# One clear instead of two behind every second indirect transfer of GpSimd, in two expert layers

## What is computed

```python
h = patches(x)                                    # 4096 x 256
h = h + attention0(layernorm(h))
h = h + experts0(layernorm(h))                    # 7 routed experts, top 2, and a shared one
h = h + attention1(layernorm(h))
h = h + experts1(layernorm(h))                    # 16 experts in 4 groups, top 4
# experts: combine[t, e] is the weight of expert e for token t, zero but for the chosen ones
out = 0
for e in range(E):
    out = out + combine[:, e:e+1] * ((silu(x @ w_gate[e]) * (x @ w_up[e])) @ w_down[e])
```

## Time and profile before

| | |
|---|---|
| runs | 1649.97, 1649.74, 1642.79 us; median 1649.74 |
| profiled execution, its own time | 1643.09 us |
| span of its profile, first to last instruction | 1641.3 us |
| mean granted TensorE clock | 0.924 of full speed |
| PE busy | 1390.6 us, 85% of the span |
| DVE, ACT, POOL busy | 1049.6, 757.0 and 661.7 us |
| clears of layer 0 (L620) | 112, 14.4 us busy |
| clears of layer 1 (L1250) | 224, 26.4 us busy |
| indirect transfers of layer 1 (L1256, L1275) | 112 scatters and 112 gathers |

### The profile page before, as it was taken

The page is one execution under the profiler, slowest core; times in us unless marked ns, Lnnn a source line. Parts: engine busy times, 40 slices in busy tenths (PEclk is TensorE's granted clock), DMA queues, the critical chain, the costliest instruction groups (busy, mean ns, idle before and its releaser), DMA issues. The chain is left out here.

```text
span 1641.3 us, 37317 instructions
## 1 busy us (share of the span) xinstructions
PE 1390.6 (85%) x14157; PEld 1222.5 (74%) x14188; DVE 1049.6 (64%) x2196; ACT 757.0 (46%) x1288; POOL 661.7 (40%) x888
## 2 busy tenths in 40 slices
PE   6979999999999976688962788899767899889882
PEld 5867888888888866688862576667567889889882
DVE  4654575476476477765665468888758766466654
ACT  5324444444444433254541566677522365556520
POOL 4015312112111005466264354333365666663665
PEclk9989999999999997899995899999857999999997
DMA  7305655325325005247651010000082377877843
GB/s 278 116 27 169 224 168 190 105 87 190 111 91 172 2 5 215 78 148 238 207 174 37 14 33 8 1 2 2 2 307 71 113 254 236 259 232 232 240 126 90
DMA packets 142885, 215.59 MB, mean 131 GB/s; under 512 B 14336, under 2 KB 112768, under 8 KB 141824
## 3 DMA queue, kind: packets, MB, share of 16 engines
q1 hardware_dynamic: 121648, 160.20, 29.5%
q0 software_dynamic: 18624, 52.45, 10.2%
q10 hardware_dynamic: 2448, 0.61, 0.2%
HBM read 103.64 MB, written 109.58 MB: 130 GB/s over the span
## 5 line engine op out<-in xcount | busy, mean ns | idle before, releaser
L125 PE MATMUL e_p_gu<-e_w_hi,e_xt_hi 128*128 (+1 forms) x676 | 202.0, 299 | 12.2 <-DVE e_xt_lo L724 8.6
L125 PE MATMUL e_p_gu<-e_w_lo,e_xt_hi 128*128 (+1 forms) x676 | 196.0, 290 | 0.0
L125 PE MATMUL e_p_gu<-e_w_hi,e_xt_lo 128*128 (+1 forms) x676 | 196.0, 290 | 0.0
L1275 POOL DMA_INDIRECT e_xn<-results,e_row_of x112 | 114.3, 1020 | 77.3 <-issue 47.9
L125 PEld LDWEIGHTS e_p_gu<-e_w_hi,e_xt_hi 128*128 128x128 f32 x676 | 134.1, 198 | 14.4 <-issue 12.4
L125 PEld LDWEIGHTS e_p_gu<-e_w_lo,e_xt_hi 128*128 128x128 f32 x676 | 134.7, 199 | 0.0
L125 PEld LDWEIGHTS e_p_gu<-e_w_hi,e_xt_lo 128*128 128x128 f32 x676 | 134.4, 199 | 0.0
L125 PE MATMUL e_p_y<-e_w_hi,e_hid_hi 128*128 (+1 forms) x338 | 113.3, 335 | 8.4 <-DVE e_hid_lo L743 7.1
L1256 POOL DMA_INDIRECT rows<-e_xn,e_row_of x96 | 94.8, 988 | 54.2 <-issue 47.2
L125 PE MATMUL a_J<-a_xt_hi,w_qk_hi 128*128 128x512 f32 x256 | 106.7, 417 | 7.4 <-DVE a_xt_lo L1960 5.4
L1942 DVE TENSOR_TENSOR a_ot_lo<-a_O,a_ot_hi 128x1024 fp32r<-128x1024 f32 x32 | 39.1, 1223 | 114.5 <-ACT a_ot_hi L1885 114.5
(11 more groups left out here) (335 smaller groups left out, 4393.9 us busy)
## 6 DMA issues: line engine op xcount, KB each, us to landing
e_moved<-rows SPq DMA_DIRECT2D x121, 256.0 KB
results<-e_y SPq DMA_DIRECT2D x121, 256.0 KB
rows<-a_zero SPq DMA_DIRECT2D x28, 1024.0 KB, 5.8
pa_x<-in_x SPq DMA_DIRECT2D x7, 1536.0 KB, 6.3
w_qk_in<-in_we SPq DMA_DIRECT2D x24, 384.0 KB, 6.3
we_parts<-w_qk_in SPq DMA_DIRECT2D x24, 384.0 KB, 2.5
we_parts<-a_e_lo SPq DMA_DIRECT2D x24, 384.0 KB, 2.4
e_w_hi<-we_parts SPq DMA_DIRECT2D x4, 1536.0 KB, 16.1
```

The lines of the kernel that those rows point to most:

```text
L125: mm = eng.matmul(out, lhs[a], rhs[b], start=start and n == 0, stop=stop and n == len(terms) - 1, skip_group_check=skip)
L1275: pool.indirect_dma_start(out=yg[g % RING][:, k, :], out_offset=None, in_=d["results"][c][0:rooms[c] * P], in_offset=bass.IndirectOffsetOn ...
```

## The change

In both stages `rest()` clears its buffer once instead of twice. The wait behind the clear stays, and a rest still stands behind every second transfer.

```diff
@@ -616,8 +616,7 @@
 
             def rest():
 
-                for _ in range(BURST):
-                    cleared(pool.memset(idle[:], 0.0))
+                cleared(pool.memset(idle[:], 0.0))
 
             def scatter(c):
                 pool.wait_ge(routed, c + 1)
```

## The result

The changed kernel took 1625.41 us, the median of four runs (1620.94 to 1627.93), beside 1649.86 us, the median of four runs of the kernel before. The ratio is 0.9873, with a 95% interval of 0.9848 to 0.9898: about 21 us faster, between 17 and 25 by the interval. The two medians lie 24.5 us apart, at the upper end of that, and the two profiled executions 18.8, because executions of either kernel differ by 7 to 8 us among themselves. The forecast was 1627 us with a range of 1618 to 1641. The profiled execution took 1624.29 us, against 1643.09 before.

What follows compares the result with a forecast made beforehand. POOL was taken to bound stretches of both layers, not the whole kernel. 124 rests at 0.16 us gave 19.8 us, so 1623.3 us from the profiled time or 1629.9 from the median; forecast 1627 us, range 1618 to 1641.

Steps and rivals of the forecast that it cites:

- The price of a rest: On POOL, each rest loses a 0.06 us gap and a 0.10 us clear: 0.16 us, bounds 0 and 0.18.
- The 0.77: On POOL, the 0.77 us from a rest's last clear to the next transfer, claimed to stay unchanged.
- the rival in which it grows to 0.93: Behind each rest, 0.77 us becomes 0.93 and the time stays at 1643 to 1650 us; chance 0.08.
- The places: Rests on POOL's path in both layers: 124 of 168 count, at 0.16 us each, 19.8 us in sum.
- 69 rests of the gathers: Rests in layer 1's gathers 0, 1 and 2 and layer 0's gather 1, at 0.16 us each, 11.0 us.
- Layer 0's two terms: 15 rests inside layer 0's scatter 1 and 15 inside its gather 1, 2.4 us each.
- the 17.58 us break: POOL's wait before layer 1's gather 1 for chunk 1's stored results, 17.00 us before; claimed not to hide gains ahead.
- Scatter 2's row numbers: Layer 1, scatter 2's start: waiting for DVE's row numbers could lose 0 to 1.3 us of 3.8; taken as 0.
- PE as the limit: Layer 1, 1376 to 1496 us: PE or stores set the pace, so only 11.0 us are gained; chance 0.09.
- Longer transfers: Gather rows, median 1003 ns, might collide more with DVE's work or its port hold; no loss counted.
- The other side: 1376 to 1580 us: indirect transfers crowd SP's loads and stores as DMA share nears 1; 1651 or 1658 us; chance 0.03.
- The start: Whole kernel: gain subtracted from the profiled 1643.1 us or the median 1649.74, giving 1623.3 or 1629.9; forecast set between.

Runs made afterwards that it cites:

- three_clears: Three clears instead of two in every rest of both layers of the kernel before: 1667.0 us, ratio 1.0121 to the kernel before.
- one_gathers: One clear behind every second gather, still two behind every second scatter, in both layers: 1635.34 us, ratio 0.9932 to the kernel before.
- one_layer0: One clear per rest in layer 0 only, layer 1 keeping two as in the kernel before: 1639.93 us, ratio 0.9956 to the kernel before.
- one_layer1: One clear per rest in layer 1 only, layer 0 keeping two as in the kernel before: 1634.69 us, ratio 0.9922 to the kernel before.
- no_rest: Changed kernel with its remaining clear and wait removed, so nothing stands between indirect transfers: 1842.6 us, ratio 1.1167 to the kernel before.
- rest3: Changed kernel with one waited clear behind every third indirect transfer instead of every second: 1701.05 us, ratio 1.0315 to the kernel before.
- late_wait: Changed kernel with its clear kept but waited for only two rests later: 1853.67 us, ratio 1.124 to the kernel before.
- paced: Changed kernel with 21 small clears behind every second transfer, waited for only two rests later: 1653.53 us, ratio 1.0043 to the kernel before.
- paced15: Changed kernel with 15 small clears behind every second transfer, waited for only two rests later: 1636.79 us, ratio 0.9944 to the kernel before.

## Why the prediction was right

*The price of a rest*, 0.16 us: right. The 0.77 stayed, so the rival in which it grows to 0.93 falls by the earlier trace rows and the chain after, and by three_clears, whose 20 us stand beside the term's 19.8. By the median turns a rest became 0.17 us shorter among the scatters of layer 1 and 0.16 among the gathers.

*The places*: 69 rests of the gathers, worth 11.0 us by the sum, gave 11.2 (0.0068 x 1647.59, interval 7 to 15) in one_gathers. Layer 0's two terms, 4.8 together, gave 5.8 in the profiles and 7 us (0.0044 x 1648.4, interval 3 to 12) in one_layer0. Gather 0's end moved gather 1's start, as the earlier trace rows said, and the 17.58 us break did not absorb the gain ahead of it.

*Scatter 2's row numbers* is the one term mis-sized. It was priced between 0 and 1.3 us and put at 0. In the profile after, scatter 1 ran from its first to its last transfer in 74.25 us for 79.10 (0.6 of these 4.9 us lie in shorter transfers, the rest in the gaps between them), but POOL then stood 4.46 us for the row numbers where it had gone on after 0.78: 3.7 us were lost, outside the bounds, and of the 3.8 us of the term 1.3 remained. A new wait at the start of scatter 2 was one of the prediction's own signs of being wrong. The reason given, that chunk 0's pairs and DVE's routing would start earlier by the same amount, failed in that run: the row numbers of chunk 2 came 78.59 us behind those of chunk 1 before, and 79.82 after. In one_layer1, with the same edit, the stretch shrank by the whole 3.9 us (77.26). What moves DVE's routing by a microsecond or two from run to run was not found. So gather 0 ended 6.2 us earlier against scatter 1, not the 9 that the prediction asked for.

*PE as the limit*: falls. The stretch from scatter 2 to gather 0's end gave 4.9 of 5.0, PE still has 8 idle us from 1412 to 1483, and DVE still waits for gathered rows.

*Longer transfers*: nearly none. The gathers' durations after (least, median, longest, for the earlier trace rows):

```profile
L1273 POOL DMA_INDIRECT e_xn<-results,e_row_of x112: 997/1007/1270, 1414.0 to 1611.7; - x112
```

The median rose from 1003 to 1007 ns, the mean from 1020 to 1027, which is 0.8 us over all 112. The Trainium skill's rule in SBUF — State Buffer, section "SBUF: two separate sides", that a DVE instruction can hold up GpSimd's descriptor making, has no visible part in the change's gain, nor in the loss of no_rest, whose scatters of layer 0 have a median of 0.98 us.

*The other side* did not come, but its reasons were the wrong ones. It asked for a DMA share near 1 and called that far away. The harm that exists has another place (ACT, DVE and PE; SP's loads too, with 82 us of waits on "remote" in no_rest for none before, but not for want of DMA time), another price (194 us with no rest) and another point: a turn of two scatters between 3.14 and 2.95 us with waited rests, while the DMA share falls (0.61 from 1400 to 1500 us in rest3, 0.41 in no_rest). The change stopped at most 0.19 us short of where it is shown to turn round. The profile of before could not show this, and that the change lands on the good side of that edge is luck: no term of the sum says where the edge is.

*The start*: the sum from the profiled time was 1623.3 and the profiled run after took 1624.29; from the median it was 1629.9, and the median after was 1625.41. The forecast of 1627 lies so close in part by luck: no row of before said where between 1643 and 1650 us to start. Later the medians of the kernel before were 1645.5 to 1648.4 us in five further sets. What was forecast by rows is the gain: 19.8 us, inside the 17 to 25 of the interval; the stretches gave 17.3.

## What to carry to other kernels

When a filler instruction stands between transfers, price it by the row, but ask what it spaces out: here the second clear was pure cost, while the time that the first one and its wait take lets the other engines run. Look for the edge by thinning and by stretching the filler, and compare the kernels by the pace that results, not by how many waits they have: a kernel that changes the wait and the pace at once (late_wait) seems to prove that a pause is needed, and a kernel near the old pace (paced) does without one. Compare like with like, too: scatters and gathers have different turns, and with the two mixed paced15 seems to have the pace of the changed kernel. And watch for waits with no releaser in the profile on engines that the edit does not touch; they were the clearest sign of this loss.

## What the runs showed of the hardware

Indirect transfers of 128 rows of 1 KB that follow each other on POOL in 1.28 us slow all other engines, with waits of up to 30 us that the profile gives to nothing (late_wait, ACT), although POOL's own rows stay at 0.97 us and the DMA engines are idle more than half of the time (a share of 0.41 from 1400 to 1500 us in no_rest); at one transfer in 1.68 us (paced) nothing of this is seen. The Trainium skill, Perfetto Trace Analysis, section "DMA Instruction — SWDGE (GPSIMD)", says that such a row ends when the descriptors have been made and not when the data have moved; the unchanged 0.97 us therefore does not exclude that something behind it piles up. What that is was not shown: no row names it. Behind a waited clear the next transfer starts after 0.77 us (one, two or three clears), behind an unwaited one after 0.19 (late_wait), behind 21 of them after 0.38 to 0.44 (paced).
